# A perceiver block with a selective scan and routed experts: three scan states placed elsewhere among norm and convolution, and the sum of the states started and ended on VectorE

## The reference

```
x = x + cross_attention(layernorm(x), ctx)      # 16 heads of 64: two tokens make one position
x = x + mamba(layernorm(x))                     # below
x = x + routed_ffn(layernorm(x))                # top 4 of 16 experts, width 256

mamba: xc    = silu(causal_conv4(x @ x_proj) + conv_b)          # 1024 channels
       delta = softplus(x @ dt_proj + b);  B, C = x @ B_proj, x @ C_proj
       for each of 16 states s, along the 64 tokens:
           h_s = exp(delta * A[:, s]) * h_s + delta * B[s] * xc
       y = sum over s of h_s * C[s]  +  D * xc                  # then y @ out_proj
```

## Time and profile before

| | us |
|---|---|
| three runs | 1289.04, 1291.8, 1298.3 |
| median | 1291.8 |
| the profiled execution's own time | 1291.31 |
| its span | 1289.4 |
| PE busy | 1128.8 (88%) |
| DVE busy | 882.7 (68%) |
| ACT busy | 623.6 (48%) |

### The profile page before, as it was taken

The page is one execution under the profiler, slowest core; times in us unless marked ns, Lnnn a source line. Parts: engine busy times, 40 slices in busy tenths (PEclk is TensorE's granted clock), DMA queues, the critical chain, the costliest instruction groups (busy, mean ns, idle before and its releaser), DMA issues.

```text
span 1289.4 us, 13313 instructions
## 1 busy us (share of the span) xinstructions
PE 1128.8 (88%) x4276; PEld 720.5 (56%) x4276; DVE 882.7 (68%) x954; ACT 623.6 (48%) x1378; POOL 134.2 (10%) x113
## 2 busy tenths in 40 slices
PE   5997879998999899999899998338999999999992
PEld 4885645764755676665477664314554445454451
DVE  1312579999678899977999995569999966133312
ACT  4542665673577466475756546224555422322220
POOL 0000111000000070000043000040000001133002
PEclk9997889999999899999999999569999999999997
DMA  8367567777500354500144140069999976999994
GB/s 290 115 212 297 209 213 236 245 247 258 190 8 18 95 179 126 157 9 17 50 129 148 44 149 6 9 241 321 377 378 365 366 276 214 379 379 407 411 362 130
DMA packets 115188, 266.27 MB, mean 207 GB/s; under 512 B 11280, under 2 KB 44208, under 8 KB 115120
## 3 DMA queue, kind: packets, MB, share of 16 engines
q1 hardware_dynamic: 99248, 207.22, 46.4%
q0 software_dynamic: 15872, 58.20, 11.8%
HBM read 197.07 MB, written 68.32 MB: 206 GB/s over the span
## 4 chain that ended last, share of the span: by engine, by line
PE 51%; DVE 32%; ACT 7%; DMA 5%; issue 3%; POOL 1%; SPq 1%; POOLq 0%; ACTq 0%; DVEq 0%
DVE state L1363 12%; PE bank L816 9%; PE bank L684 6%; PE bank L777 6%; PE bank L717 6%; DVE state L1360 6%; PE bank L696 5%; PE bank L837 4%; PE bank L795 3%; DMA queries_ctx<-in_xp_t 3%; PE bank L748 3%; DVE decay L1367 2%; DVE state L1370 2%; DVE y_acc L1374 2%; PE bank L633 2%
## 5 line engine op out<-in xcount | busy, mean ns | idle before, releaser
L1363 DVE TENSOR_TENSOR_SCAN state<-decay,state 128x2048 f32<-128x2048 f32 x64 | 283.0, 4422 | 18.1 <-ACT decay L1111 17.2
L816 PE MATMUL bank<-expert_w,block_x_t 128*128 128x512 f32 x496 | 225.8, 598 | 3.6 <-ACT block_x_t L1165 3.6
L684 PE MATMUL bank<-decay,params 128*128 128x512 f32 x384 | 172.6, 595 | 2.7 <-DVE decay L1367 2.7
L1652 POOL DMA_INDIRECT dispatched<-ffn_x,slot x32 | 74.1, 2316 | 684.2 <-DVE slot L1456 675.6
L816 PEld LDWEIGHTS bank<-expert_w,block_x_t 128*128 128x128 f32 x496 | 91.1, 194 | 94.7 <-issue 90.4
L1111 ACT ACTIVATE decay<-delta_even,params 128x256 f32<-128x256 f32 x256 | 107.2, 498 | 55.1 <-PE bank L684 52.9
L777 PE MATMUL bank<-normed_t,queries_ctx 128*128 128x256 f32 x512 | 117.1, 390 | 8.9 <-DMA queries_ctx<-in_xp_t 6.0
L717 PE MATMUL bank<-probs,ctx 128*128 128x256 f32 x512 | 117.9, 384 | 7.7 <-ACT probs L1010 7.7
L696 PE MATMUL bank<-ctx,queries_ctx 128*128 128x256 f32 x512 | 121.0, 393 | 1.2 <-issue 1.2
L1511 DVE SCALAR_TENSOR_TENSOR hidden<-hidden,bank 128x256 f32<-128x256 f32 x62 | 26.1, 421 | 137.8 <-ACT hidden L1169 123.0
L1111 ACT ACTIVATE decay<-delta_odd,params 128x256 f32<-128x256 f32 x256 | 106.2, 498 | 28.5 <-PE bank L684 25.1
(11 more groups left out here) (192 smaller groups left out, 1326.1 us busy)
## 6 DMA issues: line engine op xcount, KB each, us to landing
dispatched<-ffn_x POOLq DMA_DIRECT2D x38, 1024.0 KB, 5.6
expert_w<-in_eg_t SPq DMA_DIRECT2D x62, 512.0 KB
expert_w<-in_eu_t SPq DMA_DIRECT2D x62, 512.0 KB
expert_w<-in_ed_t SPq DMA_DIRECT2D x62, 512.0 KB
ctx<-in_ctx_t SPq DMA_DIRECT2D x32, 512.0 KB, 7.3
ctx<-in_ctx_n SPq DMA_DIRECT2D x32, 512.0 KB, 3.9
bc_bcast<-bc_scratch SPq DMA_DIRECT2D x64, 256.0 KB, 6.2
block_x<-dispatched SPq DMA_DIRECT2D x62, 256.0 KB
```

The source lines that it names most:

```text
L684: mm = pe.matmul(y_bank[c][:, :], ident, dA[(g * NS + j) % NDEC][:, c * 512:(c + 1) * 512], start=False, stop=(j == NS - 1))
L816: mm = pe.matmul(o, xbT[q % 2][:, c, :], w_gu[q % NW][:, :, c, :], start=(c == 0), stop=(c == DC - 1))
L1363: dve.tensor_tensor_scan(h, dA[n % NDEC][:, 0:sw], h, 0.0, ALU.mult, ALU.add).then_inc(scan_rd, 1)
L1652: pool.indirect_dma_start(xd[WAVE_OF[c]], bass.IndirectOffsetOnAxis(slot[:, i:i + 1].bitcast(U32), 0), fx[:, t, :], None).then_inc(dispatc ...
```

## The change

The sums of groups 0 to 2 no longer begin with `start_sum`. DVE adds `th_tmp` onto the product of state 0 (`add_skip`, after state 1), and ACT waits for that (`skip_added`) before it writes `queries_ctx` or the decays that follow. State 14's product is not summed by PE; DVE adds it onto that of state 15 (`join_states`), and PE sums that (`joined`). On PE, state 11 is summed behind the transposes of q_t instead of ahead of v, and state 13 behind the projections. ACT's decay 14 moves behind `attn_end`. On DVE, state 13 moves behind the norm, and the parts of states 14 and 15 stand between the convolution's pieces. SP's load for state 15 moves behind `load_proj`.

```diff
+JOINED = NS - 2
+PE_SUMS = [j for j in range(NS) if j != JOINED]
@@ sync
-                for s in range(NS - TAIL, NS):
-                    load_bc(g * NS + s)
+                load_bc(g * NS + NS - 2)
                 load_proj(g + 1)
+                load_bc(g * NS + NS - 1)
                 store_bc(g + 1)
@@ tensor, attn_prep
-                if g > 0:
-                    start_sum(g - 1)
@@ tensor, start_sum is gone
             def sum_state(g, j):
-                pe.wait_ge(step_done, g * NS + j + 1)
+                if j == JOINED:
+                    return
+                if j == 0:
+                    pe.wait_ge(skip_added, g + 1)
+                elif j == JOINED + 1:
+                    pe.wait_ge(joined, g + 1)
+                else:
+                    pe.wait_ge(step_done, g * NS + j + 1)
                 for c in range(NBK * GTS[g] // 512):
                     mm = pe.matmul(y_bank[c][:, :], ident, dA[(g * NS + j) % NDEC][:, c * 512:(c + 1) * 512],
-                                   start=False, stop=(j == NS - 1))
+                                   start=(j == 0), stop=(j == NS - 1))
@@ tensor, attention: ahead of v
-                if g > 0:
-                    for s in unit_states(g - 1, NUS[g] - 1):
-                        sum_state(g - 1, s)
@@ tensor, attention: behind the transposes of q_t
-                    for s in range(NS - TAIL - PRE, NS - PRE):
+                    for s in unit_states(g - 1, NUS[g] - 1) + list(range(NS - TAIL - PRE, NS - PRE - 1)):
                         sum_state(g - 1, s)
@@ tensor, end of projections
-                    for s in range(NS - PRE, NS):
+                    for s in range(NS - PRE - 1, NS):
                         sum_state(g - 1, s)
@@ scalar, attn_prep, ahead of the query copies
+                if g > 0:
+                    act.wait_ge(skip_added, g)
@@ scalar, decay_buffer_free
+                elif j == JOINED:
+                    act.wait_ge(joined, last + 1)
                 elif j < NS - 1:
-                    act.wait_ge(state_summed, n - NDEC + 1)
+                    act.wait_ge(state_summed, len(PE_SUMS) * last + PE_SUMS.index(j) + 1)
@@ scalar, the groups
                 attention_units(g + 1)
+                attn_end(g + 1)
                 scan_decay(g, NS - TAIL)
-                attn_end(g + 1)
                 projections(g + 1)
@@ vector
+            def add_skip(g):
+                h = dA[g * NS % NDEC][:, 0:NBK * GTS[g]]
+                dve.wait_ge(ys_rdy, g + 1)
+                dve.tensor_tensor(h, h, th_tmp[g], ALU.add).then_inc(skip_added, 1)
+            def join_states(g):
+                a, b = (dA[(g * NS + j) % NDEC][:, 0:NBK * GTS[g]] for j in (JOINED, JOINED + 1))
+                dve.tensor_tensor(b, b, a, ALU.add).then_inc(joined, 1)
@@ vector, the groups
                     if s > 0:
                         scan_step(g, s)
+                    if s == 1:
+                        add_skip(g)
                     if s == 1 and g >= 1:
                         route(g - 1)
...
-                for s in range(TAIL):
-                    scan_step(g, late.pop(0))
+                scan_step(g, late.pop(0))
                 add_tiles(g + 1)
                 dve.nop().then_inc(x1_rdy, 1)
                 conv_pads(g + 1)
                 norm(g + 1)
...
-                for s in range(PRE - 1):
-                    scan_step(g, late.pop(0))
-                for k in range(0, NBK, 2):
-                    if k // 2 in range(SCAN_PARTS - 1):
-                        scan_step(g, late[0], parts=(k // 2,))
-                    conv(g + 1, k)
+                scan_step(g, late.pop(0))
+                conv(g + 1, 0)
+                scan_step(g, late[0], parts=(0, 1))
+                conv(g + 1, 2)
+                scan_step(g, late[0], parts=(2,))
+                scan_step(g, late[1], parts=(0,))
+                conv(g + 1, 4)
+                scan_step(g, late[1], parts=(1,))
+                conv(g + 1, 6)
+                scan_step(g, late[1], parts=(2,))
+                join_states(g)
                 scan_inputs(g + 1)
```

More of the change, by code:

```diff
@@ L339, in perceiver_block @@
         state_summed = sem("state_summed")
+        skip_added = sem("skip_term_added")
+        joined = sem("state_joined")
         acc_rdy = sem("y_acc_copied")
@@ L672, in attn_prep @@
                 pe.wait_ge(a_free, ja.n)
-            def start_sum(g):
-                pe.wait_ge(ys_rdy, g + 1)
-                for c in range(NBK * GTS[g] // 512):
-                    pe.matmul(y_bank[c][:, :], ident, th_tmp[g][:, c * 512:(c + 1) * 512], start=True, stop=False)
             def sum_state(g, j):
-                pe.wait_ge(step_done, g * NS + j + 1)
+                if j == JOINED:
[6 more added lines that the diff above has]
+                    pe.wait_ge(step_done, g * NS + j + 1)
                 for c in range(NBK * GTS[g] // 512):
                     mm = pe.matmul(y_bank[c][:, :], ident, dA[(g * NS + j) % NDEC][:, c * 512:(c + 1) * 512],
-                                   start=False, stop=(j == NS - 1))
+                                   start=(j == 0), stop=(j == NS - 1))
                 mm.then_inc(state_summed, 1)
@@ L1084, in copy_sum @@
             def copy_sum(g):
-                act.wait_ge(state_summed, NS * (g + 1))
+                act.wait_ge(state_summed, len(PE_SUMS) * (g + 1))
                 for c in range(NBK * GTS[g] // 512):
```

## The result

Fourteen runs of each: 1302.42 us in the median after the change, 1290.67 before, the ratio 1.0089 with a 95% interval of 1.0070 to 1.0108. The changed kernel is slower by about 11.5 us. The profiled execution has a span of 1301.9 (its own time 1303.8) against 1289.4 before. PE's busy time fell only from 1128.8 to 1127.1, although six groups of eight recorded matmuls are gone, three start terms and three sums (4276 matmuls became 4228), and the granted clock over the run went from 0.946 to 0.937. Rows of the experiments carry the lines of their own file, again shifted by a few.

The account below looks back on a forecast made before the run. PE and DVE were taken to trade places as the bound, with the joints between groups deciding. Terms -2.05, -0.7, +3.05 and +4.1 gave +4.4, with +1.3 for the clock +5.7: 1291.3 to 1297 us, range 1288 to 1304.

Parts of the forecast that it names:

- J1: Joint between groups at about 290 to 420 us, from last unit's matmuls to lead states: 0.7 us faster.
- J2: Joint between groups at 510 to 635 us: 5.1 us later, less 2.05 gained in the lead, so +3.05.
- J3: Joint at 723 to 815 us, copy_sum ahead of the logarithm: DVE's use of the logarithm 4.1 us later.
- J0 and the lead: Group 0's lead (170 to 205 us) and later leads: without start_sum, scan 2 or route starts 2.05 us earlier.
- v earlier by 2.7: At a joint's start, v projection begins 2.7 us earlier because state 11's sum moves behind the transposes.
- The root behind decay 14: Norm: ACT's square root waits behind decay 14, DVE waits 5.1 us instead of 0.36; the 2.7 us are lost.
- The convolution, 26.4: DVE needs 26.4 us from first convolution piece to the end of the last, before 18.3; logarithm's use 5.4 late.
- The join costs nothing in J1 and J2: DVE's 2.3 us addition of states 14 and 15 stays hidden while ACT's chain ends last.
- The clock: TensorE's clock falls at new idle gaps, 1.8 to 2.1 us each; bounds -2.1 to +7.4, taken as +1.3.
- Rival (a): PE's projections stay the bound, joints give back what was cut: -14.4 us, 1277; chance 0.07.
- Rival (c): Clearly slower: clock falls at every new gap and the join shows too, +16.6 us, 1308; chance 0.09.
- Rival (d): ACT table switch right behind a decay costs 1.3 us beyond its load, delaying the root: 1300; chance 0.03.

Follow-up runs that it names:

- keep_warm: Changed kernel plus three unread matmuls in each of PE's two new gaps per joint, ahead of norm transposes and last sum; 1293.56 us, ratio 1.0028 to before.
- root_first: Changed kernel with ACT's square root of the norm ahead of decay 14 instead of behind it; 1288.35 us, ratio 0.9985 to the kernel before.
- balanced: root_first with state 13's input product and scan ahead of x1, and state 14 begun ahead of the first convolution piece; 1269.92 us, ratio 0.9840 to before.
- warm_norm: Changed kernel with three extra unread matmuls on PE only ahead of the norm transposes; 1297.90 us, ratio 1.0033 to the kernel before.
- idle_filled: root_first with state 13's input product and scan ahead of x1, convolution pieces ordered as in the changed kernel; 1286.09 us, ratio 0.9950 to before.
- skip_only: Kernel before with only start_sum removed, the skip term added on DVE and ACT waiting for it; 1288.42 us, ratio 0.9986 to before.

## Why the prediction came out as it did

The time, 1302.4, lies in the range of 1288 to 1304 near its upper end; the effect was forecast as +5.7 and is +11.5. The mechanism held and one term was mis-sized, the clock's. By the table of the joints, keep_warm, in which the gaps are filled, is -4.1, +2.7 and +4.1 against before in J1, J2 and J3, where the prediction without its clock term has -0.7 (-2.8 if J1's old fall goes, and it went), +3.05 and +4.1: right to 0.4 in J2 and J3, and J1 1.3 better than forecast. The changed kernel, with its gaps, is -1.8, +5.0 and +8.3.

- **J0 and the lead, -2.05 each:** right on DVE to 0.1 in J0 (scan 2), 0.9 instead of 2.05 from the logarithm to route in J1 and J2, where the slow last sum stands between. I wrote that "the sums and the scores behind them" come as much earlier. In this execution PE ran into a wait of 2.25 and a slow sum, and J0 gave nothing; over eleven executions with this lead it gave 1.7 in the mean, so this part is borne out as far as it can be told.
- **v earlier by 2.7:** right; in J1 it starts 4.41 behind the start of the last context instead of 7.08. In J2 that context was slow this time (5.41) and in J3 fast, the reverse of the earlier trace rows; nothing ties that to the change, and the table of the joints leaves it out.
- **The root behind decay 14:** right: 5.54 for 5.1, and root_first takes it back. I had it cost nothing at the transposes, since PE transposed at the same time as before. That was right for the transposes and missed what follows a gap of 2.80 where the earlier trace rows had none: a projection of 3.6 instead of 1.9, so that the x projection in J2 starts 25.05 behind the v projection instead of 23.5.
- **The convolution, 26.4:** right to 0.1. tanh waits for DVE. From tanh to the logarithm's use the text has 7.1, but its three terms add up to 7.5, and that is what the 578.8 was made with; measured 7.3.
- **The join costs nothing in J1 and J2:** right only for DVE. Sum 15 stood on the path there too, because it was slow.
- **The clock, taken at +1.3 between -2.1 and +7.4:** this is the term that failed. The falls at the two gaps in each joint cost some 8 us by the timed runs of keep_warm and 8.8 by its trace; less the 2.1 of J1's old fall, which did go (the first x matmuls ran at full clock, 10.63 for 48 after 12.70), it is +6.7, near the upper bound and not near the +1.3 taken between them. A fall came at each of the three last sums and at each of the three norm gaps. The last sums' part was bounded rightly, at 5.4; of the norm gaps, the transposes' slack was to let through at most 1.0 in J2 and J3 and nothing in J1, and it was 0.6 in J1 and in J2 and 2.5 in J3. The rows disagreed for gaps of 1.9; I left out three more of the kernel before that count against the small value, 2.59 in group 0, with a group of 5.31 behind it instead of 3.46, and two of 3.99, with 5.97 and 5.31, and one that counts for it, 2.32 ahead of the last context of J1, with 3.72. (A fall at the earlier trace rows is 5.41 - 3.72 = 1.7, not the 1.8 of the text.)
- **Rival (a)**, the projections still bound, was wrong for this order; balanced shows that it is what a better order gives. **Rival (c)** had the right ingredients: all three sums slow; what it added for the join in J1 and J2 did not show (32.51 with it and 32.47 without). **Rival (d)** falls: the load behind decay 14 is 1.28, starts 0.01 after decay 14 has ended, and the root follows 0.02 after the load. The drain that the Trainium skill (ScalarE: Activation LUTs, What ACT_TABLE_LOAD costs) adds to a switch is not seen here, nor in the earlier trace rows.

What stays open: why a gap of the same length is followed by a fall of the clock in one execution and not in the next, and why warm_norm's timed runs gain 7 us where its trace has 4 (the ratio's interval allows it).

## What to carry to other kernels

When a step is moved on one engine, read the list of every other engine that waits for it. Here decay 14 followed sum 11 behind the transposes, and the square root that the whole joint waits for stood behind decay 14; moving one call (root_first) was worth 13 us. Idle time on a second engine is not recovered by moving work out of a wait into a stretch where that engine is soon the last: count the engine's work between the first and the last thing that others wait for (26.4 us in idle_filled and 19.6 in balanced, 1.1% apart). And where the bounding engine is TensorE, a saving on it that only makes it wait can be worth less than nothing (without the join, which spares PE a sum of 3.6 in each joint, J1 and J2 are 1.75 shorter each): cost the gap as well as the work.

## What the runs showed of the hardware

A few microseconds of useless matmuls in each joint made the kernel faster by 0.6%. In the changed kernel all three gaps of 3.21 were followed by a sum with the granted clock at 0.67 to 0.69, and all three of 2.80 by a projection with 0.51 to 0.71; one of 3.13 in skip_only by a sum with 0.54. Each group took 1.6 to 3 us longer than at full clock, and each fall lasted for one or two groups of matmuls. The Trainium skill (TensorE: Matmul & The Clock Gate, The HAM clock gate) says that idle time lowers TensorE's clock and work restores it; the rows agree.

The length of the gap alone does not decide it. Over the thirteen profiled executions the last sum behind a gap of 3.20 or 3.21 was slow 7 times of 12 (never in the three joints of idle_filled), the B and C projection behind one of 2.80 was slow 8 times of 9, and the last weighted context was slow 19 times of 24 behind 1.92 to 1.94 (5.4 instead of 3.72) but only 2 times of 10 behind 2.32. What does decide it, no run here shows. So a single pair of executions can differ by several us in stretches that the change did not touch.
